# Probabilities of an attention stage transposed by DMA instead of TensorE, denominators from a ones column, stack copies by quarters, and a new order of the engines

## The reference, cut to what matters

```python
def layer(h, params):                      # twice, two sets of weights
    u = einsum('bid,bjd->bij', h, h) / sqrt(D)
    delta = softmax(u, axis=-1) * adj
    attn = delta / (sum(delta, axis=-1) + 1e-10)
    ctx = (attn * upper) @ (h @ wl.T + b_l) + diag(attn) * (h @ ws.T + b_s) + (attn * lower) @ (h @ wr.T + b_r)
    return relu(norm(ctx) * g + beta)
x = layernorm(x + layer(layer(x)))
q, k, v = heads(x @ Wq + bq), heads(x @ Wk + bk), heads(x @ Wv + bv)
scores = q @ k.T / sqrt(32) + beta * adj
scores = where(adj > 0, scores, -9e15)
probs = softmax(scores, axis=-1)
x = layernorm(x + probs @ v)
```

## Time and profile before

| | us |
|---|---|
| median of 3 runs | 1981.52 |
| lowest, highest | 1979.25, 1983.75 |
| the profiled execution | 1980.52 |
| its span, first to last instruction | 1978.8 |
| PE busy in the span | 1864.2 |
| DVE busy | 1628.7 |
| ACT busy | 1263.1 |
| POOL busy | 757.5 |

### The profile page before, as it was taken

One profiled execution on the slowest core, in us unless ns is written; L12 is line 12 of the kernel. 1 busy time (PEld: TensorE's weight loads), 2 busy tenths in 40 slices (PEclk: granted clock), 3 DMA queues, 4 the chain that ended last, 5 costly groups with the idle time before them and its releaser, 6 DMA issues.

```text
span 1978.8 us, 43612 instructions
## 1 busy us (share of the span) xinstructions
PE 1864.2 (94%) x14656; PEld 1799.2 (91%) x14656; DVE 1628.7 (82%) x5318; ACT 1263.1 (64%) x3612; POOL 757.5 (38%) x778
## 2 busy tenths in 40 slices
PE   4799999999999999999999999999999999999965
PEld 4799999999999999999999999999999999999954
DVE  4568888888888988888888888898888888888864
ACT  3356667666666766666766666676666676666644
POOL 1323443344434334343344433433434334443430
PEclk8899999999999999999999999999999999999975
DMA  4023322232322223332223332222333222333320
GB/s 146 27 73 84 89 64 58 71 89 81 83 76 65 62 78 88 82 84 66 60 67 89 81 84 78 65 61 77 89 82 83 68 67 60 87 81 83 81 49 16
DMA packets 144548, 147.18 MB, mean 74 GB/s; under 512 B 17596, under 2 KB 144328, under 8 KB 144328
## 3 DMA queue, kind: packets, MB, share of 16 engines
q1 hardware_dynamic: 133424, 131.20, 25.0%
q10 hardware_dynamic: 10904, 13.20, 1.8%
HBM read 56.25 MB, written 12.58 MB: 35 GB/s over the span
## 4 chain that ended last, share of the span: by engine, by line
PE 79%; DVE 15%; issue 2%; ACT 2%; DMA 1%; SPq 0%; POOL 0%; ACTq 0%; POOLq 0%; DVEq 0%
PE bank_w L368 40%; PE bank_m L368 10%; PE bank_u L368 7%; PE bank_p L511 7%; PE bank_o L368 5%; PE bank_s L368 5%; DVE normed L815 2%; DVE pT_lo L863 2%; DVE masked L857 2%; DVE normed L801 2%; DVE stats_y L818 2%; PE bank_t L385 1%; PE bank_u L450 1%; PE bank_t L396 1%; PE bank_t L375 1%
## 5 line engine op out<-in xcount | busy, mean ns | idle before, releaser
L656 ACT ACTIVATE prob<-masked,hmin 128x256 f32<-128x256 f32 x768 | 383.7, 503 | 73.2 <-DVE hmin L857 67.5
L857 DVE CUSTOM_DVE_ANT_0 masked<-bank_s,bias_adj 128x256 f32<-128x256 f32 x768 | 292.5, 419 | 72.1 <-PE bank_s L368 66.0
L663 ACT ACTIVATE pT_hi<-bank_p 128x512 f16<-128x512 f32 x384 | 227.9, 593 | 96.0 <-PE bank_p L511 77.6
L863 DVE TENSOR_TENSOR pT_lo<-bank_p,pT_hi 128x512 f16<-128x512 f32 x384 | 262.6, 684 | 12.7 <-ACT pT_hi L663 10.6
L511 PE MATMUL bank_p<-ident,prob 128*128 128x128 f32 x1536 | 241.5, 281 | 23.9 <-DVE pT_lo L863 23.3
L605 ACT ACTIVATE hlrh<-bank_w 128x384 fp32r<-128x384 f32 x256 | 120.9, 484 | 159.8 <-PE bank_w L368 159.8
L955 POOL TENSOR_SCALAR v_rest<-adj_in 128x512 f32<-128x512 f32 x32 | 62.1, 1940 | 397.0 <-issue 396.4
L368 PE MATMUL bank_w<-w_graph0h,hT_ach 128*128 128x384 f32 x576 | 203.8, 354 | 8.6 <-DVE w_graph0l L715 8.4
L511 PEld LDWEIGHTS bank_p<-ident,prob 128*128 128x128 f32 x1536 | 177.4, 144 | 36.8 <-issue 29.9
L368 PE MATMUL bank_w<-w_graph1h,hT_bh 128*128 128x384 f32 x576 | 200.5, 348 | 0.0
L368 PE MATMUL bank_w<-w_graph0l,hT_ach 128*128 128x384 f32 x576 | 195.5, 339 | 0.0
(11 more groups left out here) (200 smaller groups left out, 5880.3 us busy)
## 6 DMA issues: line engine op xcount, KB each, us to landing
x_in<-in_x SPq DMA_DIRECT2D x64, 384.0 KB, 3.1
adj_in<-in_adj SPq DMA_DIRECT2D x96, 256.0 KB, 3.2
q_st<-qk_hi SPq DMA_DIRECT2D x256, 96.0 KB, 2.2
k_st<-qk_hi SPq DMA_DIRECT2D x256, 96.0 KB, 2.3
q_st<-qk_lo SPq DMA_DIRECT2D x128, 96.0 KB, 2.2
k_st<-qk_lo SPq DMA_DIRECT2D x128, 96.0 KB, 2.2
out<-result ACTq DMA_DIRECT2D x32, 384.0 KB, 2.5
prob<-in_L_gnn_Wl SPq DMA_DIRECT2D x2, 192.0 KB, 3.9
```

Source lines behind the costliest of these rows:

```text
L656: nc.scalar.activation(prob[:, h % 2, i, :], masked[:, i, :], ACT.Exp, bias=hmin[:, i, h:h + 1], scale=-1.0, accum_out=hsum[:, i, h:h + 1] ...
L663: nc.scalar.activation(pT_hi[:, h % 2, :, :].rearrange("p j i -> p (j i)"), bank_p[:, :], ACT.Copy).then_inc(s_pt_hi, 1)
L857: ve.tensor_tensor_reduce(masked[:, i, :], bank_s[:, i * S:(i + 1) * S], bias_adj[:, i, :], -SCALE, BIG, ALU.add, ALU.min, hmin[:, i, h:h ...
L863: ve.tensor_tensor(pT_lo[:, h % 2, :, :].rearrange("p j i -> p (j i)"), bank_p[:, :], pT_hi[:, h % 2, :, :].rearrange("p j i -> p (j i)"), ...
```

## The change

1. **Transposes.** `prob` is no longer transposed on PE. ACT copies it as f16 into `halves[:, b, :, 0, :]`, DVE writes the difference to `halves[:, b, :, 1, :]` (both operands in SBUF now), and SP issues one transposing DMA for a head, 1,024 f16 columns of 128 partitions, into `pT` [128, 8, 128]. attend reads its stationary operands from pT. `halves` and `pT` have two buffers by k % 2.
2. **Denominators.** Each part of v gets a 33rd column, one in the first part and zero in the others. Its product is the row sum. ACT's readout (hsum) and c_sum's step on DVE are gone; DVE takes four reciprocals a partition from bank_o after each second head, 6 times a period. attend's matmuls have 99 and 66 columns.
3. **Stack copies by quarters.** The 24 copies are the same, in eight steps of three (q_stack.r, k_stack.r), each with its own semaphore; heads run in the order of `HEADS`, so the first need quarter 0 alone.
4. **Banks.** bank_p is gone, bank_s is two banks. DVE writes masked scores straight into `prob`, and exp works in place. Small tiles share one tensor (`pairs`), and the biases of both layers one row set.
5. **Order.** All lists are new, and SP has one too.

```diff
+HEADS = (0, 4, 8, 9, 1, 5, 2, 6, 10, 11, 3, 7)
...
+    "sp": """
+        weights.6-1 weights.7-1 a_x.0 c_adj.0 weights.8-1 weights.9-1 weights.10-1 weights.11-1 q_stack.0
+        k_stack.0 b_adj.0 q_stack.2 q_stack.1 a_adj.0 k_stack.1 weights.0 weights.1 b_x.0 k_stack.2 weights.2
+        weights.3 q_stack.3 k_stack.3 weights.4 weights.5""",
...
+            def stack(t, side, r):
+
+                c = t - 2
+                if r == 0:
+                    wait(sp, s_qk_lo, NC * (2 * c + side + 1))
                 for slot in range(SLOTS):
                     part = (qk_hi, (qk_lo, qk_hi)[side], (qk_hi, qk_lo)[side])[slot]
...
+                    sp.dma_start((q_st, k_st)[side][slot * HD:(slot + 1) * HD, r::HPG, :].bitcast(F32),
+                                 part[r * HD:(r + 1) * HD, side, :, :].bitcast(F32)).then_inc(s_stack["qk"[side]][r], 16)
...
+            def weights(t, k):
+
+                s = t - 2
+                sp.wait_ge(s_pt_lo, NH * s + k + 1)
+                wait(sp, s_pv, NH * s + k - 1)
+                sp.dma_start_transpose(pT[:, k % 2, :, :], halves[:, k % 2, :, :, :].rearrange("p i a s -> p (i a s)")
+                                       ).then_inc(s_pt[k % 2], 16)
...
-            def weights(t, h):
-                s = t - 2
-                pe.wait_ge(s_prob, NT * (NH * s + h + 1))
-                wait(pe, s_pt_lo, NH * s + h)
-                for j in range(NT):
-                    for i in range(NT):
-                        last = nc.tensor.transpose(bank_p[:, j * S + i * P:j * S + (i + 1) * P],
-                                                   prob[:, h % 2, i, j * P:(j + 1) * P], ident[:, :])
-                last.then_inc(s_pt, 1)
...
+            def attend(t, k):
+                s, h, b = t - 2, HEADS[k], k % 2
+                pe.wait_ge(s_pt[b], 16 * (NH // 2 * s + k // 2 + 1))
+                if k == 0:
                     pe.wait_ge(s_v_all, NT * (s + 1))
...
+                        mm(bank_o[:, at:at + VP * VC], pT[:, b, 4 * i + j, :], vp, j == 0, False)
+                        last = mm(bank_o[:, at:at + 2 * VC], pT[:, b, 4 * i + 2 + j, :], vp[:, 0:2 * VC],
                                   False, j == NT - 1)
...
+                    nc.scalar.activation(prob[:, k % 2, i, :], prob[:, k % 2, i, :], ACT.Exp, bias=hmin[:, i, k:k + 1],
+                                         scale=-1.0).then_inc(s_prob, 1)
...
+            def weights(t, k):
+
                 s = t - 2
...
+                act.wait_ge(s_prob, NT * (NH * s + k + 1))
+                wait(act, s_pt[k % 2], 16 * (NH // 2 * s + k // 2))
+                nc.scalar.activation(halves[:, k % 2, :, 0, :], prob[:, k % 2, :, :], ACT.Copy).then_inc(s_pt_hi, 1)
...
+            def weights(t, k):
+                dve.wait_ge(s_pt_hi, NH * (t - 2) + k + 1)
+                ve.tensor_tensor(halves[:, k % 2, :, 1, :], prob[:, k % 2, :, :], halves[:, k % 2, :, 0, :], ALU.subtract
+                                 ).then_inc(s_pt_lo, 1)
...
+                ve.reciprocal(hinv[:, :, a:b + 1:b - a], parts[:, :, :, HD, 0])
+                ve.tensor_reduce(att[:, :, a:b + 1:b - a, :], parts[:, :, :, 0:HD, :], AX.X, ALU.add).then_inc(s_att, 1)
```

More of the change, by code:

```diff
@@ L32 @@
 VP = 3
+VC = 33
 SLOTS = 3
@@ L218, in graph_attention_kernel @@
         bank_m = bank("bank_m")
-        bank_s = bank("bank_s")
-        bank_p = bank("bank_p")
+        bank_s = [bank("bank_s0"), bank("bank_s1")]
         bank_o = bank("bank_o")
@@ L279, in pipeline @@
                 todo = []
-                if order == "pool" and t < 3:
+                if order == "pool" and t == 2:
                     todo.append(("split", t, t))
@@ L297, in _ @@
         def _(sp):
-            def stack(c, which):
-                side = "qk".index(which)
-                wait(sp, s_qk_lo, NC * (2 * c + side + 1))
+            def stack(t, side, r):
+                c = t - 2
+                if r == 0:
+                    wait(sp, s_qk_lo, NC * (2 * c + side + 1))
                 for slot in range(SLOTS):
                     part = (qk_hi, (qk_lo, qk_hi)[side], (qk_hi, qk_lo)[side])[slot]
-                    for r in range(HPG):
-                        sp.dma_start((q_st, k_st)[side][slot * HD:(slot + 1) * HD, r::HPG, :].bitcast(F32),
-                                     part[r * HD:(r + 1) * HD, side, :, :].bitcast(F32)).then_inc(s_stack[which], 16)
@@ new lines, in c_adj, with a_x, b_adj @@
+            def c_adj(t, _k):
+                wait(sp, s_em, 2 * (layer_a(t - 1) + 1) if t <= NB
+                     else 2 * (layer_b(t - 1) + 1))
+                sp.dma_start(adj_in[:, :, :], adj_v[t - 2]).then_inc(s_adj["c"], 16)
+            def a_x(t, _k):
+                wait(sp, s_resid, (t - 1) * NT)
+                if t == 1:
+                    sp.wait_ge(s_tx_pe, NC)
+                sp.dma_start(x_in[:, :, :], x_v[t]).then_inc(s_xa, 16)
+            def b_adj(t, _k):
+                if t >= 2:
+                    wait(sp, s_badj, t - 1)
+                else:
+                    wait(sp, s_em, 2 * (layer_a(t - 1) + 1))
+                sp.dma_start(adj_in[:, :, :], adj_v[t - 1]).then_inc(s_adj["b"], 16)
@@ L352, in load, with body_and_weights @@
                                  ).then_inc(s_stage[n], 16)
[L354 to L361 removed]
+            steps = {
+                "c_adj": c_adj, "a_x": a_x, "b_adj": b_adj, "b_x": b_x, "a_adj": a_adj, "weights": weights,
+                "q_stack": lambda t, r: stack(t, 0, r), "k_stack": lambda t, r: stack(t, 1, r),
+            }
+            def body_and_weights(t, todo):
+                run(steps, todo)
+                for n in {0: (0, 1)}.get(t, ()):
+                    load(n)
+            pipeline(sp, "sp", body_and_weights)
             sp.wait_ge(s_out, 16 * NB)
@@ L638, in qk @@
                 act.wait_ge(s_qk, 6 * s + j + 1)
-                wait(act, s_stack["qk"[side]], STACKED * s)
+                if g == 0:
+                    for r in range(HPG):
+                        wait(act, s_stack["qk"[side]][r], STACKED * s)
                 nc.scalar.activation(qk_hi[:, side, g, :], bank_w[j % 2][:, 0:S], ACT.Identity,
```

259 lines of the change are left out of this document (102 added, 157 removed).

## The result

| | before | after |
|---|---|---|
| median | 1980.62 us (4 runs, 1979.25 to 1983.75) | 1995.79 us (4 runs, 1992.82 to 2005.07) |
| span of the profiled execution | 1978.8 us | 2003.3 us |
| ratio | | 1.0084 (95%: 1.0064 to 1.0104) |

The change makes the kernel 0.8% slower. The forecast was 1862 us, 134 us less. The time lies inside the range, at its far end, and the side is the wrong one.

What follows compares the result with a forecast made beforehand. The prediction took PE's work in written order as the bound, broken by waits for DVE. Its terms, -138 + 16 + 21 - 10 - 8 = -119 us, took 1980.5 to 1862 us; range 1785 to 2000, chance some 0.8.

Steps and rivals of the forecast that it cites:

- DVE, only 7 us behind: Per period: work off PE counts almost in full until DVE, busy 50.5 us against PE's 57.5, is the limit.
- -138 us for the transposes: PE's 1,536 fp32 transposes into bank_p: their 7% of the chain leaves the time, 138 us.
- +16 for the low half: DVE's low-half subtraction, now with two SBUF operands: POOL's interference adds 0.5 us a period, +16 us (0 to +72).
- +21 for the reciprocals: DVE: six small reciprocals a period at 0.16 us, less one operation dropped, counted in full, +21 us.
- Rival 3: The transposing DMA bounds the kernel, by SP's issue time or PE's stalls; times from 1980 us up; chance 0.20.
- the windows: PE's work between attend k-2 and attend k, 4.1 us at the tightest; PE stalls for what L exceeds it.
- the two rules weighed: Trainium skill on the transposing DMA: 1309 ns a block, estimated 10.5 us for eight; or 261 GB/s, estimated 1.0 us.
- 0 for L: L, the transposing DMA's time from freed buffer to landed data, taken as 3.8 us, fits under all PE windows: 0 us.
- -8 for the quarters: Program's end: last batch's first scores wait for six stack copies, not 24, 11.5 us less; net -8 us (-12 to +10).
- -10: Two banks of bank_s: PE's overlapping waits for hmin and the weight loads shrink, -10 us (0 to -17).
- the check by the period: Steady state: the period falls from 58.6 to 55.1 us, PE busy 95% of it, DVE 94%.
- rival 1: Both engines fill up: some of PE's waits go too, the period falls to 52.5 us, 1777 us; chance 0.13.

Runs made afterwards that it cites:

- no_dma: Changed kernel with four buffers of halves and no transposing DMA, attend reading halves untransposed, reciprocals replaced by additions of the same shape: 1897.71 us.
- no_dma_half: The kernel of no_dma with DVE's low half of the probabilities on 256 instead of 512 columns, attend's second product reading the high half: 1834.52 us.
- before_no_turn4: Kernel before without its 1,536 PE transposes and without a DMA for them, halves made from prob and read untransposed, four buffers of prob: 2008.40 us.
- no_dma_pool: The kernel of no_dma with POOL's L963 made to wait for the period's first hT_bl: 1857.01 us.
- pool_later: Changed kernel with one more wait: POOL's last bias step (L963) starts after the period's first hT_bl: 1972.02 us.
- recip_once: The kernel of all_three with the reciprocals of each pair of heads in the first period only: 1887.70 us.
- h4_p2: Changed kernel with four buffers of halves, two of pT as before, layer 2's weight halves sharing one tile: 1941.97 us.
- all_three: Changed kernel with four buffers of halves, k_stack.2 and q_stack.1 earlier in SP's order, and POOL's L963 waiting for the first hT_bl: 1879.55 us.

## Why the prediction was wrong

**The view of the bound.** PE at 94% and 79% of the chain was read rightly, but "DVE, only 7 us behind" was taken as a distance that must be used up before DVE counts. The runs show that it is on the path much sooner: no_dma's chain is 55% DVE at a DVE share of 86%, and no_dma_half shows that most of DVE's work there counts.

**-138 us for the transposes.** Not had in the old order: before_no_turn4 is 30 us above the kernel before, where DVE's operations are also 47 us longer. With the new order, no DMA and no collision, no_dma_pool is 123 us under it (0.9381). So the gain was seen with transposes and order changed together; how much of it is the order's by itself no run separates.

**+16 for the low half.** Right in size: 684 to 728 ns, 44 x 384 = 17 us. The median stayed at 685 ns and single ones took up to 1939, so the growth is the spread that the prediction had named as the sign of POOL. But I had looked for POOL's interference only in the instruction that changed its form. The dearer hit was on hT_bl, whose form did not change and whose place did: 24 us (pool_later). Its row of before, all executions within 3 ns, showed that nothing held it up then, not that nothing could.

**+21 for the reciprocals.** The time of one was well put, 176 ns against the 160 taken. Whether they cost anything on the path is open, as recip_once brought a collision of its own.

```profile
L881 DVE RECIPROCAL hinv<-bank_o 128x4 f32<-128x4 f32 x192 | 33.8, 176 | 21.8 <-PE bank_o L382 21.8
```

**The DMA's own numbers.** Right, and measured a little under what was taken. The transposition lands in 3.1 us (3.8 taken) and SP takes 1.25 us to issue one (1.5 taken; the shortest, median and longest of the 384 are 1.23, 1.25 and 2.38). The page's DMA issues, with the median us to landing last:

```profile
adj_in<-in_adj SPq DMA_DIRECT2D x96, 256.0 KB, 3.3
q_st<-qk_hi SPq DMA_DIRECT2D x256, 96.0 KB, 2.3
...
pT<-halves SPq DMA_TRANSPOSE x384, 3.1
```

Rival 3 names the right culprit, the transposing DMA, but by the wrong road: SP is not full, and PE's waits at bank_o are 28.8 us in all. One of them shows what the windows left out. attend.2 and attend.3 stand side by side and free both buffers of pT within 0.33 us; SP issues the two transpositions one after the other, 1.25 us each, and the second lands that much later. So attend.4 finds its data there (1034.76 us) and attend.5 waits 0.30 us (until 1035.55). The windows were compared with L alone, not with L behind another issue. The first of the two rules weighed, that of the Trainium skill in "VectorE: DVE Perf Modes", does not carry over to a DMA of eight blocks by multiplying; the measured 3.1 us are less than a third of the 10.5. The estimated 1.0 us by the second rule was for the moving alone; the 3.1 us are from issue to landing, and no run shows the moving by itself.

**0 for L.** This is the step that failed. It asked what a transposition that starts at attend k-2 does to attend k, which is the ring of pT (the buffers written and freed in turn), and compared L with what PE has to do between. `halves` has two buffers as well, and its ring is longer: attend k-2, SP's issue of k (behind stack copies, if they stand between), landing of k, ACT's hi copy of k+2, DVE's low half of k+2. I wrote "Both halves and pT have two buffers" and priced the ring of pT alone. And the engine that waits is ACT, which I had called covered by 19 us of slack a period: slack on average does not cover a wait in front of qk_hi, on which PE and DVE hang. Size: 98 us for the DMA in all (the clock's share included), 54 of them by the ring of `halves` alone (h4_p2); SP's order is worth about 41 once the ring is open.

**-8 for the quarters.** The mechanism held, most of its gain did not. Before, the last batch's first stack copy is issued at 1911.63 us and its first scores start at 1929.81, 18.2 us later. After, one line each from SP's and PE's timeline:

```profile
1944.01 0.61 SPq L312 DMA_DIRECT2D q_st<-qk_hi  x1
...
1949.54 0.71 PE L382 MATMUL bank_s<-k_st,q_st 96*128 96x256 f32 x4 [2.01 <-issue]
```

That is 5.5 us, 12.6 less, where 11.5 was forecast. But the first copy itself comes later, 10.7 us behind the batch's first q matmul (1933.34) instead of 5.2 (1906.45), since SP's queue stands at four transpositions until 1943.96. And from the first scores to the end of the program it takes 53.8 us instead of 49.0; PE waits 14.5 us for the transposing DMA at bank_o in the last 100 us. From the first q matmul to the end it is 70.0 us against 72.4: 2 us, not 8. What the quarters alone are worth was not run. Nor were the two banks of bank_s (-10); PE's wait there for hmin hardly changed (6.8 us before, 6.2 after).

**The forecast's number.** With no DMA and no collision the kernel takes 1857 us (no_dma_pool), 5 off the 1862, and all_three has the period of 55 us that the check by the period gave. Since -138 was seen only with the new order, and neither +21, -10 nor -8 is confirmed, the closeness is in part luck. What the forecast lacked is then 98 us for the DMA and its rings (after less no_dma) and 41 for the collision at hT_bl once the DMA is gone (no_dma less no_dma_pool); with the DMA in place the same wait of POOL was worth 22 to 24, so the two overlap.

**Slips in the working.** None moves the forecast. Rival 3's 1980 + 32 x 20 is 2620, not 2630. SP issues five input loads a period, not four (adj_in three times, x_in twice). And the range from 1785 does not hold rival 1's own 1777.

## What to carry to other kernels

- A transfer put between two engines closes a ring for every buffer that it reads or writes. Walk each ring through all queues, from the release to the next writer, and ask what stands behind the waiting instruction; to compare latency with the bound engine's window prices one ring only. Here four buffers ahead of the DMA were worth 54 us, four behind it a third of that. Where one queue serves two buffers freed together, add its issue time to the latency of the second.
- When an order is tuned, an edit's sign can hang on another: the same SP order cost 73 us with two buffers and gave 41 with four. Repeat such an edit once the bound is lifted.
- Work that leaves the busiest engine may have been filling its waits. Where the second engine is nearly as busy (here 86% beside 98%), test the removal by itself before counting it.
- An edit that moves or removes steps can bring a DVE operation beside a POOL one that it never met before, as in the changed kernel, before_no_turn4 and recip_once. Compare the mean of every DVE group before reading a time.

## What the hardware showed that I had not expected

- A transposing DMA of a [128 x 1024] f16 tile from SBUF to SBUF costs no more to landing than a plain load of the same bytes: 3.1 against 3.3 us; but it takes SP 1.25 us to issue. It moves in small packets: 550,037 in all after the change (144,548 before), 423,100 of them under 512 B (17,596 before), and the DMA share of a period went from 0.28 to 0.59 for 100 MB more.
- A DVE subtraction of 256 columns takes 0.43 us or 1.51, by whether a POOL operation has started beside it; a DVE operation on two columns 0.17 or 0.91 (recip_once).
- TensorE's granted clock fell to its lower level (0.50) 11 times in 1000 us of the steady state, each time behind a stretch in which PE hardly worked, and not once in the same 1000 us before the change or in all_three.
